# Attention steps rebuilt: keys projected from two-part operands and copied straight into the stacks, scores four heads ahead, projections strewn

## What is computed

```python
x = x + tanh(g_xattn[0]) * L0_attention(layernorm(x), ctx, mask)      # scores masked with -1e15
x = x + tanh(g_ffn[0])   * L0_experts(layernorm(x))                   # top 2 of 8, and a shared one
x = x + tanh(g_xattn[1]) * L1_attention(layernorm(x), ctx)
x = x + tanh(g_ffn[1])   * L1_ffn_with_lora(layernorm(x))
# an attention, for each batch and head:
q, k, v = x @ Wq + bq, ctx @ Wk + bk, ctx @ Wv + bv
softmax(q @ k.T / 4) @ v, then @ Wo + bo
```

## Time and profile before

| | |
|---|---|
| median of 3 runs | 870.8 us (870.23 to 872.3) |
| profiled execution | span 871.8 us, 22331 instructions; the three runs are the only times on record, and the span lies between the last two digits of their range |
| PE busy | 781.5 us, 90% |
| DVE / ACT / POOL busy | 580.9 / 472.6 / 213.6 us |
| mean granted TensorE clock | 0.965 of full |
| steps of layer 0, layer 1 | from about 57 to 331 us, and from about 488 to 766 us |

### The profile page before, as it was taken

One profiled execution on the slowest core, in us unless ns is written; L12 is line 12 of the kernel. 1 busy time (PEld: TensorE's weight loads), 2 busy tenths in 40 slices (PEclk: granted clock), 3 DMA queues, 4 the chain that ended last, 5 costly groups with the idle time before them and its releaser, 6 DMA issues.

```text
span 871.8 us, 22331 instructions
## 1 busy us (share of the span) xinstructions
PE 781.5 (90%) x7992; PEld 603.7 (69%) x7992; DVE 580.9 (67%) x1773; ACT 472.6 (54%) x1012; POOL 213.6 (24%) x212
## 2 busy tenths in 40 slices
PE   5879999999999888999996599999999989888996
PEld 2546777777777665689974476766776667577996
DVE  3777777777787767764545777778788667564333
ACT  2445566566555556356652355655566555654553
POOL 2553132133222406500035522422221111000000
PEclk9899999999999999899998799999999999899999
DMA  7598788868876905623327958798689887000001
GB/s 200 141 225 201 152 157 174 159 147 175 171 166 139 214 17 147 178 93 121 123 77 165 186 128 152 148 190 178 134 182 186 165 170 159 10 1 1 20 19 38
...
## 3 DMA queue, kind: packets, MB, share of 16 engines
...
...
## 4 chain that ended last, share of the span: by engine, by line
PE 56%; DMA 15%; SPq 11%; DVE 7%; ACT 5%; issue 4%; ACTq 1%; POOL 0%; DVEq 0%
PE ps L1963 18%; PE ps L2081 7%; DMA cT<-in_ctxT 6%; PE ps L2107 5%; PE ps L2130 4%; PE ps L2140 4%; DMA scr_q<-qp 4%; SPq L477 3%; DMA QS<-mp 3%; PE ps L2126 2%; PE ps L2401 2%; PE ps L2164 2%; SPq L426 2%; DMA QS<-scr_q 2%; SPq L413 2%
## 5 line engine op out<-in xcount | busy, mean ns | idle before, releaser
L1018 ACT ACTIVATE prob<-ps 128x400 f32<-128x400 f32 (+1 forms) x384 | 182.7, 500 | 95.4 <-PE ps L2130 88.8
L2107 PE MATMUL ps<-KS,QS 96*100 96x361 bf16 x512 | 166.9, 342 | 18.1 <-DMA QS<-scr_q 6.2
L1576 DVE CUSTOM_DVE_ANT_0 ps<-ps,biasq 100x361 f32<-100x361 f32 x256 | 135.3, 543 | 54.1 <-PE ps L2107 50.7
L1580 DVE TENSOR_REDUCE mx<-ps 100x1 f32<-100x361 f32 x256 | 127.0, 527 | 57.8 <-PE ps L2107 56.7
L2130 PEld LDWEIGHTS ps<-QS,KS 98*128 98x128 bf16 x1536 | 110.5, 101 | 53.0 <-issue 9.8
L2130 PE MATMUL ps<-QS,KS 98*128 98x100 bf16 x1536 | 135.2, 212 | 8.7 <-ACT prob L1018 4.4
L2081 PE MATMUL ps<-cT,wk 128*128 128x361 f32 x256 | 98.6, 496 | 17.5 <-DMA cT<-in_ctxT 9.9
L2107 PEld LDWEIGHTS ps<-KS,QS 96*100 96x100 bf16 x512 | 64.3, 127 | 54.9 <-DVE mx L1580 14.1
L728 POOL TENSOR_TENSOR kp<-kr,kp 128x722 bf16<-128x722 f32 x32 | 48.7, 1523 | 193.0 <-ACT kp L989 192.7
L2140 PE MATMUL ps<-prob,V 128*17 128x100 f32 (+1 forms) x3072 | 79.8, 252 | 0.2 <-ACT xT L909 0.2
L2140 PEld LDWEIGHTS ps<-prob,V 128*17 128x17 f32 (+1 forms) x3072 | 64.4, 98 | 11.9 <-issue 8.7
...
## 6 DMA issues: line engine op xcount, KB each, us to landing
...
```

Source lines behind the costliest of these rows:

```text
L1018: nc.scalar.activation(prob[0:KROWS[t], t, hg, :], ps[0:KROWS[t], c % 2, 0:HQ * S], ACT.Exp).then_inc(a["exp"], 1)
L1576: nc.vector.tensor_tensor_reduce(ps[0:S, banks[h % len(banks)], 0:S2], ps[0:S, banks[h % len(banks)], 0:S2], biasq[p][:, :], 1.0, -3.0e38, ...
L1580: nc.vector.reduce_max(mx[:, h:h + 1], ps[0:S, banks[h % len(banks)], 0:S2], axis=AX.X).then_inc(a["max"], 1)
L2107: mm(ps[0:S, banks[h % len(banks)], 0:S2], QS[p][0:SROWS, h, :], KS[p][0:SROWS, h * S2:(h + 1) * S2], start=True, stop=True).then_inc(a["s ...
```

## The change

- **Keys** are projected as the values are, from cTh, cTl and the two parts of the weights, `wkh` and `wkl`: six products of 362 columns for each half instead of two in fp32 of 361 (`project_k`). Only the keys of batch 0 of layer 0 stay in fp32 (`first_k`). Keys are now those of b + 2, not b + 3. The context is split a step earlier, for b + 3.
- **Stacks**: the store to DRAM and the load are gone. `k_copy` copies the pieces of a half from `kp` in SBUF into the six places of the stack, by six DMAs of 16 rows each. Its waits: `score_T` done with the half of the old stack, as before, and the piece itself. The wait for the DMA of the maxima is gone. The splitting goes by halves (`k_second`, `k3`).
- **Scores run AHEAD = 4 heads further ahead**: step b has scores 4 to 15 of batch b + 1 and then 0 to 3 of batch b + 2. PE waits for half 1 of stack b + 1 at `next_score(4)` of step b and for half 0 of stack b + 2 at `next_score(12)` of the same step.
- **Projections are strewn**: keys stand in twos between the first six groups of score_T, values in threes and sixes between the last six; `weigh` of hg 1 comes earlier. On DVE the splitting of maxima, keys and context stands between the maxima and not behind them.
- Both layers share one set of weight tiles; the values of batch 1 and others are computed earlier in the prologues.

The diff, cut to its core:

```diff
-KRUNS = [(0, 3), (3, 2), (5, 1)]
 NPIECE = 3
-NLOAD = len(KRUNS) + 1
+AHEAD = 4
...
-            def k_store(l, n):
+            def k_copy(l, n, half):
+
                 a, d, p = sa[l], sd, n % 2
-                if l == 1 or n >= 3:
-                    for half in range(2):
-                        sp.wait_ge(d["kload"][half][p], loaded(l, n - 2) if n >= 3 or (l == 1 and n == 2) else loaded(0, B - 2 + p))
-                for j in range(NPIECE):
-                    if j == 0:
-                        sp.wait_ge(a["k1"], START + KT * (n + 1))
-                    elif j == 1:
-                        sp.wait_ge(a["k2"], START + n + 1)
-                    else:
-                        sp.wait_ge(a["k3"], START + n + 1)
-                    sp.sem_inc(s_held, 1)
-                    sp.dma_start(scr_k[p, :, j].rearrange("k p n -> p k n"), kp[:, j, :, :]).then_inc(d["kst"][p], 16)
-
-            def k_load(l, n, half):
-
-                a, d, p = sa[l], sd, n % 2
-                if half == 0:
-                    sp.wait_ge(d["kst"][p], keys_stored(l, n))
-                    sp.sem_inc(s_held, 1)
                 if n > 1:
                     sp.wait_ge(a["sT"], START + NKT * NHG * (n - 2) + NKT * NHG // 2 * (half + 1))
                     sp.sem_inc(s_held, 1)
                 c = slice(half * HH * S2, (half + 1) * HH * S2)
-                for j, parts in KRUNS:
-                    sp.dma_start(KS[p][j * HD:(j + parts) * HD, c],
-                                 scr_k[p, half, 0:parts].rearrange("j (d h) n -> (j d) (h n)", h=HH)).then_inc(d["kload"][half][p], 16)
+                for part in range(NPIECE):
+                    if part == 0:
+                        sp.wait_ge(a["k1"], START + KT * n + half + 1)
+                    elif part == 1:
+                        sp.wait_ge(a["k2"], START + KT * n + half + 1)
+                    else:
+                        sp.wait_ge(a["k3"], START + KT * n + half + 1)
+                    for r in range(NST):
+                        if KPART[r] == part:
+                            sp.dma_start(KS[p][r * HD:(r + 1) * HD, c], kp[:, part, half, :]).then_inc(d["stack"][half][p], 16)
...
-            def step(l, b, u, i, has_ctx, has_k, weights=None):
-                if has_ctx and b > 0:
+            def step(l, b, u, i):
+                if 0 < b < B - 3:
                     ctx_load(l, b + 3, 1 - u, False)
-                if l == 1 and u == 0 and 2 <= b <= 12:
-                    q_store(l, b // 2 + 1)
-                if has_k:
-                    k_load(l, b + 2, 0)
+                if b < B - 2:
+                    k_copy(l, b + 2, 0)
                     q_load(l, b + 2, 0)
                     if l == 0 and b == 0:
                         q_store(l, 3)
-                    if l == 0 and weights is not None:
-                        expert_up(weights, u)
-                        expert_down(weights, u)
+                    if l == 0 and b < B - 4:
+                        expert_up(b // 2, u)
+                        expert_down(b // 2, u)
                     if l == 1 and 8 <= b < 12:
                         inner_weights(b - 8)
                     if l == 1 and b == 12:
                         outer_weights(0)
                         outer_weights(1)
+                if b < B - 1:
                     max_load(l, b + 1, 1 - u)
-                    sp.wait_ge(sd["mload"][1 - u], 16 * (i + u + 1))
-                    sp.sem_inc(s_held, 1)
-                    k_load(l, b + 2, 1)
+                if b < B - 2:
+                    k_copy(l, b + 2, 1)
                     q_load(l, b + 2, 1)
                     if l == 1 and b == 13:
                         outer_weights(2)
                         outer_weights(3)
                         for r in range(LPROD):
                             sp.dma_start(BT[r * LR:(r + 1) * LR, :], io["loraBT"]).then_inc(s_wf[1], 16)
-                if l == 0 and has_ctx:
+                if l == 0 and b < B - 3:
                     mask_load(b + 3, 1 - u, False)
-                if has_ctx:
-                    k_store(l, b + 3)
+                if l == 1 and u == 1 and b <= 11:
+                    q_store(l, (b + 3) // 2)
...
-            def k3(l, n):
+            def k3(l, n, m):
                 a = sa[l]
-                pool.wait_ge(a["k2"], START + n + 1)
-                nc.gpsimd.tensor_tensor(kp[:, 2, :, :], kr[:, :, :], kp[:, 1, :, :], ALU.subtract).then_inc(a["k3"], 1)
+                pool.wait_ge(a["k2"], START + KT * n + m + 1)
+                nc.gpsimd.tensor_tensor(kp[:, 2, m, :], kr[:, m, :], kp[:, 1, m, :], ALU.subtract).then_inc(a["k3"], 1)
...
-            def step(l, b, u, i, has_o, has_k, has_2, has_b):
+            def step(l, b, u):
+                has_o, has_b, has_2 = b > 0, b + 1 < B, b + 2 < B
                 if l == 0 and not has_b:
                     last_step0(b)
                     return
-                for h in range(H):
-                    if has_b:
-                        maxima(l, b + 1, 1 - u, h, h + 1, SBANKS)
-                    between(l, b, u, h)
-                    if has_o and h == 2:
+                for i in range(H):
+                    h = (i + AHEAD) % H
+                    if i + AHEAD < H:
+                        if has_b:
+                            maxima(l, b + 1, 1 - u, h, h + 1, SBANKS)
+                    elif has_2:
+                        maxima(l, b + 2, u, h, h + 1, SBANKS)
+                    between(l, b, u, i)
+                    if has_o and i == 1:
                         divide(l, b - 1)
-                    if has_o and h == 8:
+                    if has_2 and i == 4:
+                        k_rest(l, b + 2, 0)
+                    if has_o and i == 8:
                         add_attention(l, b - 1)
-                if has_b:
-                    split_max(l, b + 1)
-                if has_k:
-                    k_rest(l, b + 3, 0)
-                if has_2:
-                    ctx_low(l, b + 2, u)
-                if has_k:
-                    k_rest(l, b + 3, 1)
-                if has_o:
-                    stats(2 * l + 1, b - 1, sa[l]["x"], b)
-                if l == 0 and u == 0 and b >= 2:
-                    stats_end(F0, b - 2, b)
-                if l == 1 and b + 6 < B:
-                    combine(b + 6)
-                    if u == 1:
-                        pair_stats((b + 5) // 2)
+                    if has_2 and i == 9:
+                        k_rest(l, b + 2, 1)
+                    if has_b and i == H - AHEAD - 1:
+                        split_max(l, b + 1)
+                    if b + 3 < B and i == 12:
+                        ctx_low(l, b + 3, 1 - u)
+                    if has_o and i == 13:
+                        stats(2 * l + 1, b - 1, sa[l]["x"], b)
...
+            def project_k(l, n, p, m, products=range(KT * NPIECE)):
+
+                a = sa[l]
+                if 0 in products:
+                    pe.wait_ge(sc_lo, ctx_parts(l, n))
+                    pe.wait_ge(sw_lo, START + KT * (l + 1))
+                    if n > 0:
+                        pe.wait_ge(a["v_copied"], START + 2 * (n - 1) + m + 1)
+                cols = slice(m * P, (m + 1) * P)
+                for j in products:
+                    k, (wp, xp) = j // NPIECE, ((0, 0), (0, 1), (1, 0))[j % NPIECE]
+                    x = mm(ps[:, key_bank(l, n, m), 0:S2 + 1], (wkh, wkl)[wp][:, k, cols], (cTh, cTl)[xp][p][:, k, 0:S2 + 1],
+                           start=j == 0, stop=j == KT * NPIECE - 1)
+                if KT * NPIECE - 1 in products:
                     x.then_inc(a["k_ready"], 1)
...
+                def next_score(j):
+                    h = (j + AHEAD) % H
+                    n = b + 1 if j + AHEAD < H else b + 2
+                    if n < B:
                         if h % HH == 0:
-                            pe.wait_ge(d["kload"][h // HH][1 - u], loaded(l, b + 1))
-                        score(l, b + 1, 1 - u, h, SBANKS)
-
-
-                def values(t):
+                            stack_loaded(l, n, h // HH)
+                        score(l, n, n % 2, h, SBANKS)
...
-                for t in range(NKT):
-                    score_T(l, b, u, 0, t)
-                    if t < 2:
-                        next_score(2 + t)
-                last_values()
+                score_T(l, b, u, 0, 0)
+                next_score(2)
+                keys(0, (0, 1))
+                score_T(l, b, u, 0, 1)
+                next_score(3)
+                keys(0, (2, 3))
+                score_T(l, b, u, 0, 2)
+                keys(0, (4, 5))
                 if has_o:
                     turn_on(l, b - 1)
                 if l == 0 and u == 0 and b >= 6:
                     count_pair((b - 6) // 2)
-                for t in range(NKT):
-                    next_score(4 + t)
-                    score_T(l, b, u, 1, t)
+                next_score(4)
+                score_T(l, b, u, 1, 0)
```

(40 more changed lines are left out.)

515 lines of the change are left out of this document (249 added, 266 removed).

## The result

The changed kernel takes 1082.7 us, the median of five runs (1079.19 to 1100.12), beside 870.8 (867.12 to 872.3) for the kernel before: a ratio of 1.243 with an interval of 1.2371 to 1.2489. The prediction said 982 and a range to 1055. It had the sign and the mechanism, and both of its terms were too small.

The account below looks back on a forecast made before the run. PE's pace was taken to bound layer 0, with a stack's hand-over chain already as long as its cover in layer 1. Span 871.8 + 80 (hand-overs) + 31 (clock) = 983, left at 982 us; range 905 to 1055.

Parts of the forecast that it names:

- the mechanism: In each step PE waits twice for stack loads, since scores four heads ahead pull both readers toward their release.
- both of its terms: Over 14 steps of each layer: 80 us more for the hand-overs of half stacks, 31 us for lost clock.
- 2 H + M + C: Length of a step, two hand-overs plus two uncovered pieces of PE work: 20.7 us in layer 0, 19.7 in layer 1.
- H: Hand-over of a half stack, score_T's release to first score: 0.3 wake-up, 4.0 for six copy issues, 3.6 landing; 7.9 us.
- M: Uncovered PE work from next_score(4) to the sixth group of score_T: 2.2 us in layer 0, 1.7 in layer 1.
- C: Uncovered PE work from next_score(12) to the twelfth group of score_T: 2.7 us in layer 0, 2.2 in layer 1.
- 20 to 23 us named as the sign of being right: Step length in steps 1 to 14 that, with two PE waits a step, would show the forecast right.
- The clock term: PE drops to 1.2 GHz after its waits, slowing M and C; a quarter of 123 us taken, 31 us.
- The slow-clock rival: M and C at half clock nearly throughout, or landings of 5 us: 1030 to 1075 us; chance 0.17.
- Prologues at nothing, plus or minus 3 us: In the prologues, a store and landing saved against six more issues in SP's queue: no net change, 3 us either side.
- Keys, 1.9 us in place of 2.4: Key projection on PE, 12 products at 0.16 us instead of 4 fp32 ones: 0.5 us less a step, hidden under waits.
- The sum of 885: Total in us if the query load landed after the skill's estimated 2.4 us, making H 6.7; not adopted.

Follow-up runs that it names:

- room in the ring: Changed kernel with five half stacks of keys and queries used in turn instead of four halves, query load issued ahead of the six copies: 912.1 us, 1.055 times before.
- the ring with early keys: Changed kernel with five half stacks in turn, keys projected a step earlier, ScalarE's context and key work behind exponentials: 900.0 us (1.037); without loads 888.5 us (1.024).

## Why the prediction was wrong

- **The mechanism was right.** Two waits in nearly every step, ahead of next_score(4) and next_score(12), 52 where some 56 were named, PE at 80%, six copies and the query load in the place given, and a step of 2 H + M + C: 25.0 and 24.4 us by the table, 25.1 and 24.5 measured. That is above the 20 to 23 us named as the sign of being right, so H and the clock were mis-sized. No loads, no loss (0.984); room in the ring, and more than three quarters of the loss is gone (1.055).
- **The term at fault: H = 0.3 + 4.0 + 3.6 = 7.9 us.** It measured 9.0 in the mean. Of the 1.1 us some 0.3 are issues (the query load goes out 4.6 us behind the release in the mean, since an issue sometimes takes up to 2.2 us), and 0.8 are the landing: from the issue of the query load to the score that reads it 4.4 us pass in the mean and 4.2 in the median, and in the 14 hand-overs where its landing is on record the score starts 0.04 us behind it. "Issued over 4.0 us, the copies leave less queued ahead of it than three loads issued in 1.3 us did" was the step that failed. Copies issued every 0.64 us land every 0.9, so what is queued grows through all six; the earlier trace rows had shown 4.2 as the median, and I took the shortest landing of a copy instead. Twice a step over 28 steps: 2 x 1.1 x 28 = 62 us.
- **The clock term: a quarter of M and C.** They took 3.4 + 3.7 and 3.7 + 2.7 us where I had 2.7 + 2.2 and 2.2 + 1.7 for full clock: 14 x (2.2 + 2.5) = 66 us, in place of 31. So 35 us more. With the wait filled they take 2.7 + 2.4 and 2.3 + 2.0, so some 57 of the 66 are the clock, nearly half of the 123 that half clock throughout would cost, and 9 are work that I had counted short. The slow-clock rival, 0.17, came nearest with its 1030 to 1075. The Trainium skill, "TensorE: Matmul & The Clock Gate", section "What's actually happening", by which the throttled state is the default and activity lifts it, stood behind that rival; the window at 0.50 right behind a wait of 2.3 us agrees, and so does the clock of 0.959 with the waits filled.
- **Prologues at nothing, plus or minus 3 us.** 33.4 us of the loss lie outside steps 1 to 13. Some 15 of them are the two further steps that the count of 28 has (with the first wait for a stack, 3.48 us ahead of the score at 82.92), and 18 remain. Without loads the start is still 6.8 us later than before, and the stretch between the windows isn't longer at all, so some 11 of the 18 seem to hang on the loads too; in the prologue of layer 1, for one, PE waits 3.53 us (until 612.89) for a query load that takes 6.9 us to land.
- **The miss as a whole.** By the profiled execution it is 115 us: 62 for H, 35 for M and C, 18 outside. By the medians it is 101 us. Which of the three terms is smaller in the executions without a profile isn't shown; their mean clock is higher by 0.013 to 0.019.
- **Keys, 1.9 us in place of 2.4:** mis-sized, without effect. In the step shown above two of the twelve products start at 250.59 and 250.84 and the score behind them at 251.00: the second takes the 0.16 that I had taken, the first 0.25. Strewn in twos they cost 0.41 a pair and 2.5 for twelve, as much as before. That the rest of the order is free was right: without the loads it gains 1.6%.
- **The range** ended at the middle of the slow-clock case. The two misses go up together: with H at 9.0 us the clock costs 57 us, and with H at 6.5 (three of six copies) M and C together are within 0.4 us of my figures for full clock. I had added them as if one could be high while the other was low.
- **The fixed cost** in the Trainium skill, "DMA: Bandwidth & Descriptors", section "Anatomy of one DMA — SWDGE (gpsimd) path" (an estimated 2.4 us for the query load), was rightly set aside. Behind the copies no query load of the kernel after whose landing is on record took less than 3.2 us. The sum of 885 that I gave for it leaves out the 31 us of the clock; with them it is 915.

What stays open: why packets take longer when two queues share the engines (84 and 110 ns against 43), why they lengthen in the second half of a hand-over with six whole copies (41 to 131 ns), and which part of the ring with early keys costs its 2.4% without loads.
